# Two transformer seams reordered: feed-forward buffers moved, tiles 4-7 prepared inside the first chunks, the next layer's q/k weights split inside the last chunks

## The reference

```python
for i in range(L):                                   # L = 2
    xn = layer_norm(x, ln1_scale[i], ln1_bias[i])
    heads = retention(xn, Wq[i], Wk[i], Wv[i], gammas)   # scores = q k' * decay, no softmax
    y = group_norm(heads, gn_scale[i], gn_bias[i], H)
    tmp = xn @ Wg[i]
    x = tmp * sigmoid(tmp) * y @ Wo[i] + x
    xn2 = layer_norm(x, ln2_scale[i], ln2_bias[i])
    x = gelu(xn2 @ ffn_w1[i]) @ ffn_w2[i] + x
```

## Time and profile before

| | us |
|---|---|
| median of 3 executions (1808.08 to 1811.35) | 1808.55 |
| profiled execution | 1806.73 |
| its span | 1804.9 |
| busy: TensorE matmul / VectorE / ScalarE / GpSimd | 1677.1 / 1099.8 / 854.8 / 466.4 |

### The profile page before, as it was taken

One profiled execution on the slowest core, in us unless ns is written; L12 is line 12 of the kernel. 1 busy time (PEld: TensorE's weight loads), 2 busy tenths in 40 slices (PEclk: granted clock), 3 DMA queues, 4 the chain that ended last, 5 costly groups with the idle time before them and its releaser, 6 DMA issues. The chain is left out here.

```text
span 1804.9 us, 26236 instructions
## 1 busy us (share of the span) xinstructions
PE 1677.1 (93%) x9152; PEld 1438.6 (80%) x9152; DVE 1099.8 (61%) x2213; ACT 854.8 (47%) x1192; POOL 466.4 (26%) x340
## 2 busy tenths in 40 slices
PE   5999999999998599989998999799975999999997
PEld 4899999999998388768886887687864888888886
DVE  5445555555554666653336666634337999999995
ACT  3444444444343423253334222533324788888884
POOL 0344444443443244300002443300001121212121
PEclk9899999999999799989999999799986999999999
DMA  4111011001100410013324000132323234545622
GB/s 162 48 36 36 24 35 35 30 28 35 35 24 0 141 48 0 1 59 98 99 71 159 24 0 1 59 95 92 126 99 126 83 116 163 174 163 179 254 73 64
DMA packets 35215, 139.61 MB, mean 77 GB/s; under 512 B 4753, under 2 KB 5393, under 8 KB 28433
## 3 DMA queue, kind: packets, MB, share of 16 engines
q1 hardware_dynamic: 29984, 126.75, 19.8%
q0 software_dynamic: 5168, 12.06, 3.4%
HBM read 227.92 MB, written 12.85 MB: 133 GB/s over the span
## 5 line engine op out<-in xcount | busy, mean ns | idle before, releaser
L1730 DVE TENSOR_TENSOR e_w<-e_raw,e_w 128x2048 fp32r<-128x2048 f32 x138 | 311.2, 2283 | 14.7 <-ACT e_w L1591 14.7
L1591 ACT ACTIVATE e_w<-e_raw 128x2048 fp32r<-128x2048 f32 x138 | 264.0, 1917 | 46.4 <-DMA e_raw<-in_we 21.2
L80 PE MATMUL bank<-e_w,e_xT 128*128 128x512 f32 x1104 | 273.8, 397 | 1.4 <-DVE e_xT L1748 1.4
L80 PEld LDWEIGHTS bank<-e_w,e_xT 128*128 128x128 f32 x1104 | 206.1, 190 | 43.5 <-DVE e_xT L1748 1.8
L80 PE MATMUL bank<-ctx,wk 128*128 128x258 f32 x1536 | 195.3, 287 | 3.5 <-PEq L195 3.5
L1324 PE MATMUL bank<-fw,hh 128*128 128x512 f32 x768 | 189.0, 396 | 9.9 <-DVE hh L1182 9.9
L80 PE MATMUL bank<-x2T,fw 128*128 128x512 f32 x768 | 189.3, 396 | 6.3 <-DVE fw L1133 6.3
L80 PEld LDWEIGHTS bank<-ctx,wk 128*128 128x128 f32 x1536 | 189.5, 192 | 3.6 <-issue 3.6
L80 PE MATMUL bank<-wv,ctx 128*128 128x512 f32 x768 | 189.2, 395 | 0.0
L1324 PEld LDWEIGHTS bank<-fw,hh 128*128 128x128 f32 x768 | 146.3, 191 | 42.1 <-issue 10.5
L80 PEld LDWEIGHTS bank<-x2T,fw 128*128 128x128 f32 x768 | 146.5, 192 | 37.6 <-issue 6.7
(11 more groups left out here) (238 smaller groups left out, 2725.9 us busy)
## 6 DMA issues: line engine op xcount, KB each, us to landing
e_raw<-in_we SPq DMA_DIRECT2D x143, 1024.0 KB
fraw<-in_wf SPq DMA_DIRECT2D x64, 512.0 KB, 3.4
ctxraw<-in_ctx SPq DMA_DIRECT2D x32, 514.0 KB, 3.3
wraw<-in_wa SPq DMA_DIRECT2D x20, 512.0 KB, 5.0
X<-in_x SPq DMA_DIRECT2D x2, 1024.0 KB, 6.7
acc_d<-X SPq DMA_DIRECT2D x8, 256.0 KB, 9.1
xh_d<-A SPq DMA_DIRECT2D x8, 256.0 KB, 8.5
out<-acc_d SPq DMA_DIRECT2D x4, 512.0 KB, 5.8
```

Of the source, the lines that this page charges most:

```text
L80: last = nc.tensor.matmul(out, lhs(t, a), rhs(t, b), start=start and n == 0, stop=n == len(steps) - 1)
L1591: nc.scalar.activation(w[pos][:, 0, :, :], raw[pos][:, :, :], ACT.Copy).then_inc(m["w_hi"], 1)
L1730: nc.vector.tensor_tensor(w[pos][:, 1, :, :], raw[pos][:, :, :], r(w[pos][:, 0, :, :]), ALU.subtract).then_inc(m["w_lo"], 1)
```

## The change

The feed-forward buffers get other places. `wq` and `wk` stay uncovered, `x2T` lies over `wv` and `wg`, `fw` over the small attention buffers behind `wo`, and `hf32` and `hh` have places of their own. Waits on the last readers of the covered buffers are added (`g_ps`, `qk_ok`, `s_ps`, `o_ps`, `sws_ok`, `cen_ok`). In seams 1 and 3 both first `up` stand right behind the projection of tile 6, the last group norm is cut in two (`group_centre`, `group_scale`), and tiles 4 to 7 are prepared inside chunks 3 to 7. In seam 2 weight pieces 0 to 3 and the first tile are split inside the last two chunks. Context lines are cut, and twelve blanks of indentation:

```diff
 EARLY = 6
-X2_BANK = (1, 2, 3, 4, 5, 2, 3, 2)
+X2_BANK = (1, 2, 3, 1, 2, 2, 2, 2)
+LATE_AT = 4
...
         sw = sba("sw", [P, D])
+        pf = sba("pf", [P, 2, DC, P])
         sws = sba("sws", [P, 2, D])
-        pf = sba("pf", [P, 2, DC, P])
...
         yT = sba("yT", [P, 2, DC, P], F32R)
+        hf32 = [sba(f"hf32_{i}", [P, 512]) for i in range(2)]
+        hh = [sba(f"hh{i}", [P, 2, 512], F32R) for i in range(2)]
...
         sbf = holder(ff)
+        sbf("under_wq_wk", [P, 2, 2, DC, D])
+        fraw = [sbf(f"fraw{i}", [P, 2 * D]) for i in range(FS)]
         x2T = sbf("x2T", [P, 2, DC, TOK], F32R)
-        fraw = [sbf(f"fraw{i}", [P, 2 * D]) for i in range(FS)]
+        sbf("under_wo", [P, 2, DC, D])
         fw = [sbf(f"fw{i}", [P, 2, 2 * D], F32R) for i in range(FS)]
-        hf32 = [sbf(f"hf32_{i}", [P, 512]) for i in range(2)]
-        hh = [sbf(f"hh{i}", [P, 2, 512], F32R) for i in range(2)]
...
-            if j == 4:
-                act.wait_ge(m["down_ps"], 2 * FC * layer + FS)
+            if j == 4 and layer > 0:
+                act.wait_ge(m["up_ps"], 2 * FC * layer)
...
-        weights_hi(0)
-        weights_hi(1)
-        act.wait_ge(m["gn_in"], 32 * layer + 32)
-        norm_hi(n0, 0, bank[2])
+        if layer == 0:
+            weights_hi(0)
+            weights_hi(1)
+            act.wait_ge(m["gn_in"], 32)
+            norm_hi(n0, 0, bank[2])
...
                 if begin:
-                    for j in range(2, 8):
+                    for j in range(2 if layer == 0 else 4, 8):
...
             nc.scalar.activation(x2T[:, 0, :, t * P:(t + 1) * P], xf[t % 2][:, :, :], ACT.Copy).then_inc(m["x2_hi"], 1)
+        act.wait_ge(m["g_ps"], n0 + 8)
...
         norm2_hi(2)
+        weights2_hi(0, 2 * FC * layer)
         norm2_hi(3)
-        act.wait_ge(m["g_ps"], n0 + 8)
-        weights2_hi(0, 2 * FC * layer)
-        act.wait_ge(m["y_turned"], n0 + 8)
-        turned_hi(yT[:, 0, :, :], bank[6]).then_inc(m["yT_hi"], 1)
+        act.wait_ge(m["qk_ok"], 4 * (n0 + 8))
         weights2_hi(1, 2 * FC * layer + 1)
-        norm2_hi(4)
-        norm2_hi(5)
...
             nc.scalar.activation(hf32[k % 2][:, :], bank[k % 2][:, :], ACT.Gelu_apprx_tanh).then_inc(m["h_ok"], 1)
-        act.wait_ge(m["wo_ps"], n0 + 8)
-        for k in range(FS):
-            hidden_hi(k, 2 * FC * layer + k)
-            weights2_hi((k + 2) % FS, 2 * FC * layer + k + 2)
-            if k in (1, 2):
-                norm2_hi(5 + k)
+        for c in range(2 * FS):
+            hidden_hi(c % FS, 2 * FC * layer + c)
+            if c == 0:
+                act.wait_ge(m["s_ps"], n0 + 8)
+            if c == 1:
+                act.wait_ge(m["o_ps"], n0 + 8)
+                act.wait_ge(m["sws_ok"], 2 * (n0 + 8))
+            weights2_hi((c + 2) % FS, 2 * FC * layer + c + 2)
+            if c == 0:
+                act.wait_ge(m["y_turned"], n0 + 8)
+                turned_hi(yT[:, 0, :, :], bank[2]).then_inc(m["yT_hi"], 1)
+            if LATE_AT <= c:
+                norm2_hi(c - LATE_AT + 4)
         loops = 2 * FC // FS - 1 if layer < L - 1 else FC // FS
-        with act.Fori(1, loops) as it:
+        with act.Fori(2, loops) as it:
...
                 weights2_hi((k + 2) % FS, n + 2)
+            elif layer < L - 1:
+                weights_hi(2 * c - 4 * FC + 4, layer + 1)
+                weights_hi(2 * c - 4 * FC + 5, layer + 1)
...
                 nc.scalar.activation(xf[t % 2][:, :, :], bank[2][:, :].rearrange("p (c n) -> p c n", c=DC), ACT.Copy).then_inc(m["xr_ok"], 1)
+        if layer < L - 1:
+            act.wait_ge(m["gn_in"], 32 * (layer + 1) + 32)
+            act.wait_ge(m["down_ps"], 2 * FC * (layer + 1))
+            norm_hi(n0 + 8, 0, bank[2])
...
-        weights_lo(0)
-        norm_lo(n0, 0)
-        weights_lo(1)
+        if layer == 0:
+            weights_lo(0)
+            norm_lo(n0, 0)
+            weights_lo(1)
...
-        def group_norm(n):
...
+        def group_centre(n):
...
             nc.vector.tensor_scalar(gve[:, :], gmv[:, :, 1], 1e-6, None, ALU.add).then_inc(m["gve_ok"], 1)
...
+        def group_scale(n):
...
                 begin, end = first and k == 0, last and k == 1
-                if begin:
+                if begin and layer == 0:
...
                 if not begin:
-                    group_norm(n)
+                    group_centre(n)
+                    group_scale(n)
...
         norm2_apply(3)
-        group_norm(n0 + 8)
+        group_centre(n0 + 8)
...
         norm2_lo(2)
+        weights2_lo(0, 2 * FC * layer)
         norm2_lo(3)
-        weights2_lo(0, 2 * FC * layer)
-        norm2_apply(4)
-        norm2_apply(5)
-        dve.wait_ge(m["yT_hi"], n0 + 8)
-        turned_lo(yT[:, 1, :, :], bank[6], yT[:, 0, :, :]).then_inc(m["yT_lo"], 1)
+        group_scale(n0 + 8)
         weights2_lo(1, 2 * FC * layer + 1)
-        norm2_lo(4)
-        residual(n0 + 7, 7, bank[7])
-        norm2_aggregate(range(EARLY, NT))
-        norm2_lo(5)
-        norm2_apply(6)
-        norm2_apply(7)
...
+        def late(c):
...
+            if c == 0:
+                dve.wait_ge(m["yT_hi"], n0 + 8)
+                turned_lo(yT[:, 1, :, :], bank[2], yT[:, 0, :, :]).then_inc(m["yT_lo"], 1)
+            if c == 1:
+                residual(n0 + 7, 7, bank[3])
+                norm2_aggregate(range(EARLY, NT))
+            if LATE_AT - 1 <= c < 2 * FS - 1:
+                norm2_apply(c - LATE_AT + 5)
+            if LATE_AT <= c:
+                norm2_lo(c - LATE_AT + 4)
...
-        def chunks(n, ahead=True, tiles=False, first=None):
+        def chunks(n, ahead=True, first=None, finish=False, begin=None):
...
                     weights2_lo((k + 2) % FS, n + k + 2)
-                if tiles and k in (1, 2):
-                    norm2_lo(5 + k)
+                if begin is not None:
+                    late(begin + k)
+                if finish and layer < L - 1 and k >= 2:
+                    weights_lo(2 * k - 4, layer + 1)
+                    weights_lo(2 * k - 3, layer + 1)
...
             if half == 0:
-                chunks(b, tiles=True)
+                chunks(b, begin=0)
+                chunks(b + FS, begin=FS)
...
             else:
-                with dve.Fori(1 - half, FC // FS - half) as it:
+                with dve.Fori(2 * (1 - half), FC // FS - half) as it:
...
             if half == 1:
-                chunks(b + FC - FS, False)
...
                     norm_apply(n0 + 8, 0)
+                chunks(b + FC - FS, False, finish=True)
+                if layer < L - 1:
+                    norm_lo(n0 + 8, 0)
...
-        pe.wait_ge(m["xh_ok"], n0 + 1)
-        turn(xh[0], bank[2]).then_inc(m["x_turned"], 1)
+        if layer == 0:
+            pe.wait_ge(m["xh_ok"], 1)
+            turn(xh[0], bank[2]).then_inc(m["x_turned"], 1)
...
             pe.wait_ge(m["xh2_ok"], n0 + t + 1)
-            if t >= 5:
-                before = {5: 1, 6: 2, 7: 5}[t]
+            if t >= 3:
+                before = {3: 0, 4: 2, 5: 4, 6: 5, 7: 6}[t]
...
-        def chunks(n, half, begin=False, end=False, first=None):
+        def late(c):
...
+            if c == 0:
+                pe.wait_ge(m["yT_lo"], n0 + 8)
+                products(nc, bank[3][:, :], range(DC), lambda c, h: yT[:, h, c, :],
+                         lambda c, h: wo[:, h, c, :]).then_inc(m["wo_ps"], 1)
+            if LATE_AT - 1 <= c < 2 * FS - 1:
+                turn2(c - LATE_AT + 5)
...
+        def chunks(n, half, begin=False, end=False, first=None, c0=0):
...
             for k in range(FS):
-                if begin and half == 0 and k == 0:
+                if end and half == 1 and k == FS - 1 and layer < L - 1:
+                    pe.wait_ge(m["xh_ok"], n0 + 9)
+                    turn(xh[0], bank[2]).then_inc(m["x_turned"], 1)
+                if begin and half == 0 and k == 0 and c0 == 0:
...
                     up(n + k + 1, 0, 1)
-                if begin and half == 0 and k in (1, 2):
-                    turn2(5 + k)
+                if begin and half == 0 and c0 + k == 0:
+                    pe.wait_ge(m["cen_ok"], n0 + 8)
...
                     pe.wait_ge(m["ffn_ok"], n0 + 4 + 1)
-                down(n + k, k, begin and k == 0, end and k == FS - 1)
+                down(n + k, k, begin and k == 0 and c0 == 0, end and k == FS - 1)
+                if begin and half == 0:
+                    late(c0 + k)
...
         project_out(n0 + 7)
-        pe.wait_ge(m["y_ok"], n0 + 8)
-        turn(y, bank[6]).then_inc(m["y_turned"], 1)
-        wait_alone(pe, m["x2_lo"], n0 + 4)
+        pe.wait_ge(m["x2_lo"], n0 + 4)
...
         up(2 * FC * layer, 0, 0)
-        turn2(4)
-        turn2(5)
-        project_out(n0 + 8, bank[7])
         up(2 * FC * layer + 1, 1, 0)
-        pe.wait_ge(m["x2_lo"], n0 + 5)
-        pe.wait_ge(m["res_ok"], n0 + 9)
+        pe.wait_ge(m["y_ok"], n0 + 8)
+        turn(y, bank[2]).then_inc(m["y_turned"], 1)
...
                 chunks(b, half, begin=True)
```

(17 more changed lines are left out.)

1 line of the change is left out of this document (removed).

## The result

The changed kernel took 1799.59 us (median of 4 runs, 1799.04 to 1803.37), the kernel before 1809.27 us (median of 4) beside it: ratio 0.9947, 95% interval 0.9935 to 0.9959. It is 9.7 us faster. The forecast was 15.8 us faster, 1792.8, with a range of 1788 to 1799: the sign was right, the size was not, and the time lies just outside the range. The profiled execution took 1803.37 us, the longest of the four (span 1801.6 us, mean granted clock 0.964).

The account below looks back on a forecast made before the run. TensorE, busy 93% of the span, sets the pace except at three seams, where it waits mainly for VectorE and loses clock. Savings of 4.8 + 3.4 + 7.6 = 15.8 us from 1808.55 gave 1792.8, range 1788 to 1799.

Parts of the forecast that it names:

- rival 5: All 64 chunks: `fw`, `x2T` or `hh` slower in their new places; 0.5 us a chunk would give 1825; chance 0.05.
- Seam 1: Layer 0, retention to feed-forward: first `up` 0.8 us earlier, no wait for the first hidden block; 4.8 us saved.
- rival 1: Seams 1 and 3: clock stays low through the second `up` at both; 4.8 us back, 1797.6; chance 0.12.
- Seam 2: Feed-forward to next retention: VectorE's additions start earlier, so next tile's statistics and the gate product come 3.4 us earlier.
- Seam 3: Layer 1, retention to feed-forward: same waits go, GpSimd's additions move under chunks 2 to 4; 7.6 us saved.
- 2: Chunks 3 and 4 behind seam 3: GpSimd's additions make VectorE late; 1.8 to 3.6 us back; chance 0.08.
- 3: Seam 2: last gelus wait for weight piece 1; last hidden block 2.5 us later, total 1795.0; chance 0.08.
- 4: Behind the seams: a wait returns, ScalarE or VectorE held by the turn of `y`; half the gain, 1800.6; chance 0.05.

Follow-up runs that it names:

- the unread products: Matmuls whose result nobody reads put into TensorE's waits at seams 1 and 3, in the changed kernel with the small statistics buffers allocated last: 1787.91 us, ratio 0.9882.

## Why the prediction was right or wrong

**The step that failed** is the one that gave the new homes of the buffers no price in the sum. It stood as rival 5, "If `fw`, `x2T` or `hh` were read or written slower where they now lie, all 64 chunks would pay", with "Nothing in the profile shows that the place matters". It came true at 0.105 us a chunk, below the 0.25 at which it would have decided the sign, and took 6.7 of 15.8 us; its sign of being wrong, chunks above 5.44 us, is the one that showed. Of the three buffers it is `hh` alone, by its offset from `fw`. The mechanism was in the forecast as all or nothing: 0.5 us or nothing. A bound of 0 to 0.25 us a chunk belongs in the range, which would then have reached to 1808.8. The trace of before held a sign of it, though not in the mean durations:

```profile
L80 PE MATMUL bank<-wv,ctx 128*128 128x512 f32 x768 | 189.2, 395 | 0.0
...
L80 PE MATMUL bank<-r_wv,xn 128*128 128x512 f32 x192 | 48.1, 399 | 0.2 <-DVE r_wv L1017 0.2
...
L80 PE MATMUL bank<-r_wk,xn 128*128 128x512 f32 x192 | 46.1, 389 | 0.0
```

`wv` x `ctx`, whose slices start 1032 bytes apart and never lie alike, stands at 395 ns between two products that do lie alike. The distances from start to start do part them: `wv` x `ctx` and `wo` x `yT` (64 bytes off) never settle at 227 ns, the products of the two layers that lie alike do.

**Seam 1** was forecast 4.8 and gave 3.2. All waits went as worked out. Mis-sized were the terms of the clock: 4.41 + 2.72 for the two `up` was 8.41 in the changed kernel's profile, and 7.9 to 8.4 in eight others with this code. That is rival 1 (clock stays low through the second `up`) in part, at about 1.3 us instead of 2.4. The projection ahead of them, not counted at all, took 5.38 instead of 4.20, but 5.17 in the second profile of before too. The granted clock of 0.63 and the unread products show that it is the clock: with them the two `up` take 6.1 us, 0.2 of that a wait, at 1.00.

**Seam 2** was forecast 3.4 and gave, by the traces, 4.0 behind the last `down` less 0.9 ahead of it: 3.1, and 3.7 against the kernel with this part put back. So the size held, by two errors that partly cancel. "VectorE is full from there on, so q's 3.8 us are not the gain" held: q starts 4.8 us earlier (3.78 instead of 8.55 us behind the start of the last `down`), the gate 4.0 to 4.4. The start of the additions was taken 4.2 us behind the last `down` (968.8 against 964.6), with pieces 2 and 3 rounded 1.4 behind it; it came 3.6 behind (970.34 against 966.70), with the rounding done at 967.63, 0.9 behind. Against this, the last `down` itself was counted as late by the turn alone (0.4), and a wait for `hh` came on top.

**Seam 3** was forecast 7.6 and gave 6.8 against the first profile of before, 7.4 against the mean of three. The changed kernel's own profile has 7.17 us for the two `up`; eight profiles of other kernels with the same code there have 8.2 to 8.5, where 5.13 + 2.72 was forecast, so rival 1 cost about 0.5 us here. The additions under chunks 2 to 4 cost nothing, as said.

**Rivals.** 1 came in most executions, with 1.3 us at seam 1 and 0.5 at seam 3 instead of 2.4 each. 2 was refuted (no wait in chunks 2 to 5). 3 came, small: beyond the two products and the turn, the last `down` of layer 0 is 0.2 to 0.9 us late in all ten profiles with that code, where 2.2 was its price. 4 did not come. 5 came, at a fifth of the 0.5 us that it named.

**What the forecast could not know**: the first profile of before was 3.1 us short in the router's tail. It had no part in the sum, as that was of differences at the seams.

By the Trainium skill, "TensorE: Matmul & The Clock Gate", section "Step-by-step: what each phase is for", TensorE has two independent SBUF read ports, so loading the next weights takes no read bandwidth from the running matmul. The page says nothing of addresses, but by that sentence one would not look for a cost in the place of `hh` against `fw`. Here there is one, 226.7 against 231 to 236 ns for a matmul, and the measurement decides: either the two reads do meet somewhere, or something else in a matmul's start depends on their addresses. No run here tells these apart, and why a slow block reaches into the first six matmuls of the `up` behind it stays open too.

## What to carry to other kernels

When a buffer moves, work out its start against that of the operand it is multiplied with; keep stationary and moving operand alike modulo 256 bytes, for instance by allocating odd-sized small buffers last. This is shown for 512-column float32 matmuls (type F32R), at the offsets in the table. To see whether it is so, compare the start-to-start distances of single matmuls at full clock, well behind the start of a block: 2.80 against 2.72 us a block can't be seen in the mean duration (396 ns for `down` before and after) and costs 0.4% of this kernel. And when TensorE must wait a few us in front of a critical chain, work that nobody reads can hold the clock, as at both seams here; count its time, so that it ends inside the wait. Take two profiles of the kernel before, since a stretch of one can be 3 us off by itself.

## What the hardware showed that was not expected

- 64 free bytes ahead of one buffer made a kernel 5.2 us slower (ratio 1.0029, interval 1.0018 to 1.0040). Offsets of 64, 96, 128 and 160 bytes modulo 256 between `hh` and `fw` all cost about the same, 0.076 to 0.089 us per `down` of twelve matmuls; 0, 256 and 512 nothing.
- Two idle times of 1.31 and 1.17 us ahead of it went with a projection of 4.99 us instead of 3.01, although twelve products at full clock ended some 7 us earlier. The granted clock over it was 0.56.
- 24 products of 8 columns in a row took 2.74 us in one profile of the kernel before and 5.13 in the other, at a granted clock of 0.88 and 0.50 over that stretch.
